# Router logits of a first stage moved from TensorE to GpSimd products and VectorE sums

## The reference

```python
x = x + tanh(g_xattn[0]) * L0_xattn(ctx, layernorm(x), ...)      # per batch: 8 heads, 376 keys
h = layernorm(x)                                                  # "x2h" in the kernel
probs = softmax(h @ Wr + br)                                      # Wr: 256 x 8 experts
topk_p, topk_e = top_k(probs, 2)
pos = cumsum(one_hot(topk_e)) - one_hot(topk_e)                   # place among the expert's tokens, per batch
keep = pos < 40
buf[(topk_e * B + b) * 40 + min(pos, 39)] += h * keep             # rows sent to the experts
x = x + tanh(g_ffn[0]) * experts(buf)...
```

## Time and profile before

| | |
|---|---|
| median of 3 runs | 2261.21 us (2253.23 to 2261.25) |
| profiled execution, own time | 2261.54 us |
| its span | 2259.8 us |
| PE busy, whole span | 2198.2 us (97%) |
| DVE / ACT / POOL busy | 1615.2 (71%) / 1292.9 (57%) / 642.3 (28%) |
| mean granted PE clock | 0.992 |

### The profile page before, as it was taken

How to read it: one execution, slowest core, us unless ns; L and a number is a source line. 1 busy time by engine, 2 the same in 40 slices (tenths; PEclk the granted TensorE clock), 3 DMA queues, 4 the chain that set the end, 5 groups by cost and what they waited for, 6 DMA issues and landing times. The chain is left out here.

```text
span 2259.8 us, 49398 instructions
## 1 busy us (share of the span) xinstructions
PE 2198.2 (97%) x15486; PEld 1871.1 (83%) x15486; DVE 1615.2 (71%) x5729; ACT 1292.9 (57%) x3251; POOL 642.3 (28%) x1162
## 2 busy tenths in 40 slices
PE   9999999999999999999999999999989999999997
PEld 6777777777777777777689999999978888888886
DVE  5667677677677676777665555555579999999986
ACT  6676776776766767767533343343245555555553
POOL 1123222232232222322320000000255555555541
PEclk9999999999999999999989999999999999999999
DMA  5431111111111111111142222221222222222210
GB/s 195 136 102 45 54 44 47 53 45 47 53 36 53 44 46 54 45 47 38 40 142 72 80 85 84 67 85 47 82 59 65 64 64 63 64 68 64 64 38 19
DMA packets 136226, 146.70 MB, mean 65 GB/s; under 512 B 23090, under 2 KB 122665, under 8 KB 135840
## 3 DMA queue, kind: packets, MB, share of 16 engines
q1 hardware_dynamic: 122825, 122.13, 17.3%
q0 software_dynamic: 12288, 21.21, 3.5%
q10 hardware_dynamic: 855, 0.19, 0.1%
HBM read 101.04 MB, written 54.79 MB: 69 GB/s over the span
## 5 line engine op out<-in xcount | busy, mean ns | idle before, releaser
L735 ACT ACTIVATE a_prob<-a_prob,a_nmax 128x376 f32<-128x376 f32 x512 | 309.8, 607 | 143.8 <-DVE a_nmax L881 143.8
L881 DVE CUSTOM_DVE_ANT_0 a_prob<-a_score,a_mask_row 128x376 f32<-128x376 f32 x512 | 270.4, 543 | 92.3 <-PE a_score L1157 84.6
L1472 ACT ACTIVATE e_hidden<-e_first,keep_b 128x256 f32<-128x256 f32 x320 | 134.4, 472 | 283.0 <-PE e_first L80 282.4
L80 PE MATMUL e_second<-e_w,e_hidden 128*128 128x256 f32 x1920 | 239.5, 284 | 0.0
L80 PEld LDWEIGHTS e_second<-e_w,e_hidden 128*128 128x128 f32 x1920 | 232.6, 192 | 0.0
L1166 PE MATMUL a_turned<-keep_ident,a_prob 128*128 128x128 f32 (+1 forms) x1536 | 216.7, 277 | 1.1 <-DVE a_probT L901 0.7
L1166 PEld LDWEIGHTS a_turned<-keep_ident,a_prob 128*128 128x128 f32 (+1 forms) x1536 | 173.5, 142 | 41.0 <-issue 26.8
L743 ACT ACTIVATE a_probT<-a_turned 128x384 f32<-128x384 f32 x256 | 125.8, 492 | 127.6 <-PE a_turned L1166 127.6
L901 DVE COPY a_probT<-a_turned 128x384 f32<-128x384 f32 x256 | 141.1, 551 | 78.4 <-PE a_turned L1166 75.4
L1157 PE MATMUL a_score<-a_kT,a_qT 64*128 64x376 f32 x1024 | 196.4, 501 | 0.6
L177 POOL TENSOR_SCALAR r_var<-r_mv 128x2 f32<-128x2 f32 x64 | 12.3, 192 | 569.8 <-issue 502.4
(11 more groups left out here) (238 smaller groups left out, 5180.9 us busy)
## 6 DMA issues: line engine op xcount, KB each, us to landing
a_share<-shares SPq DMA_DIRECT2D x256, 64.0 KB, 2.6
w_in<-W SPq DMA_DIRECT2D x32, 512.0 KB, 4.2
slots<-a_zeros SPq DMA_DIRECT2D x8, 1280.0 KB, 8.6
keep_rows<-slots SPq DMA_DIRECT2D x40, 256.0 KB, 4.1
answers<-e_y SPq DMA_DIRECT2D x40, 256.0 KB, 2.2
a_xn<-x SPq DMA_DIRECT2D x32, 256.0 KB, 3.2
a_xr<-x SPq DMA_DIRECT2D x32, 256.0 KB, 3.3
shares<-a_rden_rows SPq DMA_DIRECT2D x512, 0.5 KB
```

The costliest lines, as they stand in the source:

```text
L80: last = nc.tensor.matmul(out, stationary(a, t), moving(b, t), start=start and n == 0, stop=stop and n == len(todo) - 1)
L735: nc.scalar.activation(prob[:, u % 4, a], prob[:, u % 4, a], ACT.Exp, bias=nmax[:, u % 4, a:a + 1], scale=-1.0, accum_out=den[:, u % 4, a: ...
L881: nc.vector.tensor_tensor_reduce(prob[:, u % 4, a], score[SCORE_AT[u][a]][:, 0:NKV], mask_row[:, p], -1.0, 3.0e38, ALU.add, ALU.min, nmax[ ...
L1472: nc.scalar.activation(hidden[:, 2 * j + i], first[:, j, i * CH:(i + 1) * CH], ACT.Relu, bias=b1[:, 2 * j + i, bass.ds(e, 1)]).then_inc(re ...
```

## The change

The logits are no longer a matrix product (but for batch 31, which keeps the old path in the second stage). Per batch POOL does eight `weigh`: x2h times the column of Wr for one expert, a copy of which stands in every partition (`wr_rows`), a 128x512 product; then, after a wait for that product, it adds the upper half of each row to the lower, 128x2x128. DVE `logit_part` sums the remaining 128 of each row, and `logits_sum` adds the bias. There are four product buffers, so `weigh` e waits for `logit_part` e-4. On DVE parts 0 to 3 stand at the end of step b+3, parts 4 to 7 at the start of step b+4, `logits_sum` ahead of `out_stat`; `choose`, `counts_in` and `place` stand some 10 to 20 instructions later than before. On PE `router_turn` and `router_logits` go and `router_count` takes the place of `router_turn`. On POOL both halves of a `dispatch` belong now to batch s-5: the first behind `norm1`, the second behind `norm2`. SP loads `wr_rows` at the start, and loads the second half of W2 and the bias b2, whose space the products use, at the end of the stage.

```diff
+    def weigh(eng, b, p, e):
+        if e == 0:
+            eng.wait_ge(x2h_ok, QT * (b + 1))
...
+        at_least(eng, part_ok, E0 * b + e + 1 - len(weighed))
+        both = weighed[e % len(weighed)]
+        nc.gpsimd.tensor_tensor(both, x2h[:, p], wr_rows[:, :, e].unsqueeze(1).to_broadcast([P, QT, D]),
+                                ALU.mult).then_inc(product_ok, 1)
+        eng.wait_ge(product_ok, E0 * b + e + 1)
+        nc.gpsimd.tensor_tensor(both[:, :, 0:D // 2], both[:, :, 0:D // 2], both[:, :, D // 2:D],
+                                ALU.add).then_inc(weighed_ok, 1)
+    def logit_part(eng, b, e):
+        eng.wait_ge(weighed_ok, E0 * b + e + 1)
+        nc.vector.reduce_sum(lgr[:, :, e], weighed[e % len(weighed)][:, :, 0:D // 2], AX.X).then_inc(part_ok, 1)
+    def logits_sum(eng, b):
+        eng.wait_ge(part_ok, E0 * (b + 1))
+        nc.vector.tensor_tensor(lg[:], lgr[:], br[:].unsqueeze(1).to_broadcast([P, QT, E0]), ALU.add).then_inc(soft, 1)
...
@@ SP
+                     (r["wr_rows"], t["Wr0"].partition_broadcast(P))]
...
+                if isinstance(s, int) and s == B + 2:
+                    eng.wait_ge(part_ok, E0 * (B - 1))
+                    load_w2(1)
+                    eng.wait_ge(weighed_ok, E0 * (B - 1))
+                    eng.dma_start(keep["b2"][:], t["b2"].partition_broadcast(P)).then_inc(keep["biases_in"], 16)
@@ POOL
                 if routed(s - 5):
-                    dispatch(eng, s - 5, q, range(QT, QT * 2))
+                    dispatch(eng, s - 5, q, range(QT))
                 if live(s):
                     norm0(s)
                 if here(s - 3):
                     norm2(eng, s - 3)
-                if routed(s - 4):
-                    dispatch(eng, s - 4, p, range(QT))
+                if routed(s - 5):
+                    dispatch(eng, s - 5, q, range(QT, QT * 2))
                 if live(s - 2):
                     residual(s - 2, p)
+                if here(s - 3):
+                    for e in range(E0):
+                        weigh(eng, s - 3, q, e)
@@ DVE (four of the places)
+                if here(s - 4):
+                    logit_part(eng, s - 4, 7)
                 if live(s - 1) and not (isinstance(s, int) and s == 1):
                     kvin_low(s - 1, q, 1)
                 if here(s - 4):
-                    choose(eng, s - 4, 6)
+                    logits_sum(eng, s - 4)
                 if live(s - 3):
                     out_stat(s - 3)
                 if here(s - 4):
-                    choose(eng, s - 4, 7)
+                    logits_shift(eng, s - 4)
@@ PE
-                if here(s - 3):
+                if routed(s - 4):
...
-                    router_turn(eng, s - 3, q, bank_b)
+                    router_count(eng, s - 4, bank_b)
```

More of the change, by code:

```diff
@@ L345, in router_logits @@
     def router_logits(eng, b, bank=values):
[L346 to L348 removed]
+        eng.wait_ge(rT_out, 1)
         for i in range(QT):
@@ L371, in routing @@
         "x1_stat": x1_stat, "logits_in": logits_in, "logits_shift": logits_shift, "choose": choose,
-        "counts_in": counts_in, "place": place, "router_turn": router_turn, "router_logits": router_logits,
+        "weigh": weigh, "logit_part": logit_part, "logits_sum": logits_sum, "weighed_ok": weighed_ok, "part_ok": part_ok,
+        "wr_rows": wr_rows, "weighed": weighed, "counts_in": counts_in, "place": place, "router_turn": router_turn, "router_logits": router_logits,
         "router_count": router_count, "rT_out": rT_out,
@@ L401, in attend @@
         store, rsqrt, norm1, norm2, dispatch = (r[n] for n in ("store", "rsqrt", "norm1", "norm2", "dispatch"))
[L402 to L405, removed]
+        x1_standardise, router_exp = (r[n] for n in ("x1_standardise", "router_exp"))
+        out_norm, x1_stat, weigh, logit_part, logits_sum, logits_shift, choose, counts_in, place = (r[n] for n in (
+            "out_norm", "x1_stat", "weigh", "logit_part", "logits_sum", "logits_shift", "choose", "counts_in", "place"))
+        router_count, weighed_ok, part_ok = (r[n] for n in ("router_count", "weighed_ok", "part_ok"))
         stage_kv = keep["w1_in"]
@@ L546, in load_w1, with load_w2 @@
                     eng.dma_start(stage_kv[:, n], t["W1"][0, n * P:(n + 1) * P]).then_inc(keep["w1_loaded"], 16)
[L547 to L553, removed]
+                load_w2(0)
+                eng.dma_start(keep["b1"][:], t["b1"]).then_inc(keep["biases_in"], 16)
+            def load_w2(n):
+                half = slice(n * KH // 2, (n + 1) * KH // 2)
+                eng.dma_start(keep["w2_in"][:, half],
+                              t["W2"][0, n * HID // 2:(n + 1) * HID // 2].rearrange("(k p) d -> p k d", p=P)) \
+                    .then_inc(keep["w2_loaded"][n], 16)
             def load_rows(g):
@@ L986, in step @@
                 if here(s - 4):
-                    choose(eng, s - 4, 4)
+                    logit_part(eng, s - 4, 6)
                 if live(s - 1) and not (isinstance(s, int) and s == 1):
@@ L1020, in step @@
                     turned_out(s - 2, 4, 1)
+                if here(s - 4):
+                    choose(eng, s - 4, 6)
                 if here(s - 3):
                     x1_stat(eng, s - 3, q)
[L1023 to L1024 removed]
+                if here(s - 4):
+                    choose(eng, s - 4, 7)
                 if live(s - 1):
                     row_max(s - 1, q, 0, 0)
[L1027 to L1030 removed]
                     row_max(s - 1, q, 0, 1)
[L1032 to L1033 removed]
                 if live(s - 2):
                     attended(s - 2, 1)
[L1036 to L1038 removed]
                     turned_out(s - 2, 5, 1)
@@ L1070, in step @@
                     turned_out(s - 1, 0, 1)
+                if here(s - 3):
+                    logit_part(eng, s - 3, 2)
+                if live(s - 1):
                     row_max(s - 1, q, 4, 0)
+                if live(s - 1):
                     row_max(s - 1, q, 4, 1)
+                if here(s - 3):
+                    logit_part(eng, s - 3, 3)
             all_steps(eng, step)
@@ L1229, in step @@
                     turn_prob(s - 2, 2)
-                if routed(s - 4):
-                    eng.wait_ge(v_ok, 3 * (s - 1))
-                    router_count(eng, s - 4, bank_b)
                 if live(s - 2):
```

109 lines of the change are left out of this document (60 added, 49 removed).

## The result

The changed kernel takes 2416.45 us (median of four runs, 2412.04 to 2418.28), the kernel before 2260.88 in the same comparison: ratio 1.0694 [1.0667, 1.0721], slower by 156 us. Forecast were 2358 (2264 to 2412): the direction is right, the size is not, and the time lies 4 us above the range.

The account below looks back on a forecast made before the run. PE was taken to bound the kernel before, at 34.60 us a step. 27 full steps at 3.4 us longer (+92), first steps -4 and the end +9 made +97: 2358 us, range 2264 to 2412.

Parts of the forecast that it names:

- hidden products: Rival: POOL's products near their lower end, PE takes their place in the ring: 35.0 us a step, 2277 us; chance 0.14.
- Scatters not felt: Rival: second scatter half landed when ACT comes; 33.3 us a step with full products, 2231 us; chance 0.12.
- The ring: Loop from one batch's x2h to the next through POOL, DVE and scatters: 37.0 us, 38.0 with the overlap.
- Steps 3 and 4: DVE from out_stat to the end of stat, 9.5 us; then POOL's norm0 and norm2, 4.0 us.
- steps 5 and 6: Moved scatters, issued behind norm2, until landed, 3.8 us; then ACT's x1_standardise, 1.2 us.
- Step 1: POOL's eight weigh, product and add at 2.20 us an expert: 17.7 us (13.3 to 22.1).
- the overlap: POOL's products stopped by DVE instructions with two SBUF inputs: 1.0 us a step, between none and 2.2.
- Step 2: DVE from the last logit_part through logits_sum, ahead of out_stat: 0.8 us.
- the clock: Rival: PE's clock falls behind the new gap of 4 to 5 us: 40.0 us a step, 2412 us; chance 0.12.
- Likeliest case: The ring with the overlap bounds the step: 38.0 us a step, 2358 us; chance 0.48.
- First steps: The first two routed steps, before the wait for landed scatters begins, are freer by 2.2 us each: -4 us.
- The two last intervals and the stage's end: First stage's end: +7 us for products, last sum, W2 load and later x2h; two short steps +2 us.

Follow-up runs that it names:

- e3: Changed kernel with all four scatters of a batch ahead of norm0 and POOL's products on only 8 of 256 columns: 2199.84 us, 0.9741.
- e15: e6 with parts 2 to 4 of place moved later on VectorE, behind row maxima of groups 3 and 4: 2203.98 us, 0.9747.
- e2: Changed kernel with POOL's products and adds on only 8 of 256 columns, scatters still behind norm2: 2305.56 us, 1.0204.
- e1: Changed kernel with all four scatters of a batch issued behind norm1, ahead of norm0: 2290.03 us, 1.0139.
- e6: e1 with Wr turned once at the start into contiguous rows, so products read it without the stride of eight: 2225.39 us, 0.9845.
- e7: e1 with the last logit_part and logits_sum moved behind out_stat on VectorE: 2295.00 us, 1.0160.
- e14: Changed kernel, scatters behind norm2, each product replaced by three one-input POOL passes and each add by one: 2434.07 us, 1.0772.
- e4: Kernel before, logits still on TensorE, with only the scatters moved as in the change (two behind norm1, two behind norm2): 2337.27 us, 1.0337.
- e16: e15 without POOL's adds, VectorE summing all 256 columns of each product: 2268.76 us, 1.0037.

## Why the prediction was right in direction and short in size

*Right.* PE sheds nearly all of its 2.19 us (steps of 32.6 to 32.8 in e3 and e15, forecast 32.41). x1_standardise waits for the scatters behind norm2 (3.23 us; x2h written 5.3 us behind norm2's end), v_out behind it and PE for v_out. The term "hidden products", 35.0 a step, is e2's 35.3 at the full clock. "Scatters not felt" with full products, 33.3, compares with e1's 34.7; this is not the products' size alone, since PE waits there for an a_vo that a held row maximum delays (e15), which no term of mine had.

*The ring, 38.0 forecast, 38.7 measured at the full clock.* Steps 3 and 4 together were 13.5 and took 13.1; steps 5 and 6 were 5.0 and took 5.4 (0.63 us pass ahead of the first scatter, where I had 0.1). Step 1 with the overlap was 18.7 (8 x 2.20 is 17.6, where I wrote 17.7) and took 19.0. There the split was wrong: the eight products of that step add up to 12.8 us, where I had 10.4. The stride, which I took as free, makes 1.7 of that (1.51 at least, against r_xb's 1.30), stops on POOL 0.7, where I had 1.0; the waits between the sixteen are 0.3, not 1.3. The add, 0.74 by estimate, is 0.73. Step 2 was 0.8 and took 1.2. Over 27 steps the 0.7 make 19 us.

*The step that failed: the clock.* I gave that rival 0.12, "against it: in the steady steps, gaps of 0.74 left the clock at 1.00, and I have none of 4 to 5 in a busy stretch". That was no evidence against it, only the want of a row. The gap came shorter than forecast, 2.3 to 3.9 us, and the clock still fell to 0.50 behind it; half the steps are long, and in each of these `out_stat` waits for PE's `output`, as the rival had it. My sum had nothing for this; it is +32 us. The mean of all 28 steps from 178.23 to 1296.27 is 39.9, and the time 2416, against the rival's 40.0 and 2412; as the rival had every step at 40.0 and the steps are of two lengths, that this comes so near is partly chance. Likeliest case and rival are not two cases but one, in turn: the ring makes the gap, the clock falls behind most of the gaps, and where it stays low longer PE closes the step in POOL's place.

*Left out: VectorE's share of the stops.* "DVE's own share of such stops I leave out, since it has idle time while the products run." By the groups from 300 to 900 us its operations are held 4.4 us a step in the changed kernel (a_att 4 x 0.32, sidx 1.05, the mask row 0.70, at_b 0.68, slot_s 0.47, kept 0.23), 6.0 in e1 and 2.4 in e6. One row of the changed kernel, in ns, where the kernel before has a mean of 160:

```profile
L340 DVE TENSOR_TENSOR r_at_b<-r_oh,r_slot x32: 184/934/1401, 122.0 to 1329.6; 128x32 f32<-128x32 f32 x32
```

It hid the waits that I expected at the last parts. With early scatters VectorE's list is as long as the ring (e7), and through ACT a held operation keeps PE waiting (e1, e15). The Trainium skill, "SBUF — State Buffer", section "SBUF: two separate sides", says that of a GpSimd operation that reads SBUF and a VectorE operation with two SBUF inputs, or one in a two-port mode, whichever starts first has the shared ports for its whole instruction. I weighed this for POOL. The runs agree, but with the engines exchanged: POOL's products mostly stay within 0.2 us of their shortest, while sidx, with two inputs, goes from 0.15 to as much as 1.50 us. Of the held operations kept, slot_s and the mask row have one input; in which mode they ran no run shows.

*The edges.* First steps: I gave back 4 us, and they cost 0.85. The two last intervals and the stage's end were 9 and took 14.1; later stages gave 3 back. With 19 and 32 this makes up the distance: 97 + 19 + 32 + 5 + 5 - 3 = 155.

*Open.* How much of the 2.5 us of a long step is the clock's alone and how much VectorE's being held in the same step is separated only in part. In the eight long steps at 0.92 the last a_att ahead of `output` takes 1.57 to 1.61 us against 1.00 to 1.10 in the short ones, but it also starts some 2.4 us later; in the five at 0.88 it takes 0.64 to 0.81, and these steps are the longest (41.4 to 42.0). So this operation's holding is 0.6 at most. Without holding the price is 1.5 (e2); in e14, where POOL is longer still, lower clocks (0.92) cost nothing. No run takes away the lower clock alone.

## What to carry to other kernels

Before moving an issue, follow what waits for its landing: two scatters behind the instruction that feeds their consumer cost 77 us alone (e4) and 126 together with the products (e1), and ahead of it nothing. Work given to a free engine can be paid a second time on the engine beside it (4.4 to 6.0 us a step of VectorE here): look at which of its short operations stand ahead of something that a third engine waits for, and try them elsewhere. It has to be measured each time: the same move gained 21 us in e15 and lost 45 in e16. When a step becomes longer than the busy engine's list, give the lower clock behind the new gap a term in the sum, and compare it with the time that the longer ring leaves over (nothing lost in e14, 1.5 us in e2, 2.5 here).

## What was not expected of the hardware

A 128x512 product on POOL takes 1.52 us with one operand at a stride of eight elements and 1.29 without (medians of the w_in buffers). The one-input form of the same size takes 0.62. A 128x4 operation on VectorE went from 0.17 to 1.45 us (in the median of e1) beside products of 1.5 to 1.7, and a filled gap did not save the clock, as it fell behind the next one, to 0.56 in the mean of that stretch.
